# A macaron block of two mixtures of experts and a Mamba mixer: the odd pairs' sums are added to the even pairs' sums by an accumulating DMA, and the steps of the slots get a new order

## The chip, the cores and the metric

One core of one Trainium2 chip runs the whole program. The metric is the device time in microseconds; the median of the runs counts. The engines are TensorE (PE; its weight loads are PEld), VectorE (DVE), ScalarE (ACT), GpSimd (POOL) and SyncE (SP), which only issues transfers here.

## The reference

x is 16 sequences of 256 tokens of 128 values, all in fp32.

```python
x = x + 0.5 * ffn(layernorm(x))      # 8 experts 128 -> 512 -> 128, silu, top 2 of a softmax
x = x + attn(layernorm(x))
x = x + 0.5 * ffn(layernorm(x))      # the same weights

def attn(x):
    x1 = x + mamba(rmsnorm(x, norm1_w))
    out2 = memory_attend(mamba(rmsnorm(x1, norm2_w)))
    return x1 + out2

def mamba(x):                        # 256 channels, 16 states
    xm, res = split(x @ in_w.T + in_b)
    xm = silu(conv4(xm) + conv_b)
    delta = softplus(dt(xm)); Bm, Cm = parts(xm @ xp_w.T)
    h = h * exp(delta * A) + delta * xm * Bm     # a scan over 256 steps
    y = sum over the 16 states of h * Cm
    return ((y + xm * D_ssm) * silu(res)) @ out_w.T + out_b
```

What matters here is `y`: a sum over 16 states of products of 256 channels by 256 steps, plus `xm * D_ssm`.

## The kernel before

The 16 sequences go in 8 groups of two. Each sequence passes through Mamba twice, so a group has four scans. The time of one scan is a **slot**: 32 slots, q = 4g + i. Slots 0 and 1 of a group are the first pass of its two sequences, slots 2 and 3 the second. Beside the scan of its own sequence a slot does the end of the scan before it (its **tail**), the start of the next one (its **head**), and pieces of the experts' work for other groups: 35 pieces (transposing a chunk of sorted tokens T, first layer U, second layer D) are shared between slots 0 and 1 for one call of the experts, and between 2 and 3 for another. The first call and the last (`start`, `finish`) use every expert on every token instead.

In a slot the 16 states are taken as 8 pairs j of 128 x 1024 values (2 states x 2 halves of the channels x 256 steps). For a pair: ScalarE makes the decays (`d`, line 977; line 993 `e` scales the input of the odd pairs), TensorE spreads B and C over the partitions (`t`, `k`), VectorE forms the input of the even pairs (`b`, line 1332), scans (`s`, lines 1345 and 1351) and multiplies by C (`g`, line 1363). The products of pairs 0 and 1 are written to the tiles `acc[b]` and `odd[b]`, b = i % 2; those of pairs 2 to 7 go to three buffers G in turn. GpSimd adds each of these by an accumulating DMA of 512 KB: `a2`, `a4`, `a6` to `acc`, `a3`, `a5`, `a7` to `odd` (`pair_sum`, lines 1605 and 1608), each after the one before it on the same tile has landed. `skip` makes xm * D_ssm and adds it to `odd` too. The semaphores `q_even` and `q_odd` count the landings; `landed(q, j)` names the value for pair j.

In the next slot VectorE closes the tail with the step `gate` (`gate_y`, line 1366):

```python
dve.wait_ge(*landed(q, 6))
dve.wait_ge(*landed(q, 7))
V.tensor_tensor(acc[b], acc[b], odd[b], ALU.add)       # line 1370, 128x1024
V.tensor_tensor(yg, acc[b][:, 0], acc[b][:, 1], ALU.add)
V.tensor_tensor(yg, yg, sres[b], ALU.mult)
```

then TensorE projects `yg` (`out`, or `m1` to `m4` with the memory step), and VectorE adds the residual (`xsum` or `xb`). A product of pair j waits until its buffer G is free again, which is when the pair sum three before it has landed.

The routing of an experts' call stands in slots 1 and 3: `fstats` (VectorE), `froot` (GpSimd), `fnorm`, `fturn` (TensorE), `fxT` (ScalarE), `fgate` (TensorE), `flog ftop`, `fcount` (TensorE), `fplace`, which ends with the positions `posi` (line 1239). Then GpSimd scatters the tokens to DRAM in eight indirect DMAs (`sc0` to `sc7`, line 1560). In the same slots the call before comes to its end: ScalarE's last leaf F24 copies the last results to `ys` (line 898), SyncE stores them (line 407), GpSimd gathers them in eight indirect DMAs (`ga0` to `ga7`, line 1572, the first waits for all results), and VectorE adds the weighted sum `fsum` (line 1256) as the last step of the slot. `fkeep` is a copy of a tile on GpSimd (line 1553), `rms`, `lnx` and `rmsx` are small roots, `rs` a residual.

Every engine does its instructions in order. That order is written out by hand as the table `ORDER`: for each engine four strings, one for each slot of a group, of the names above (`p2`: two pieces; `F3`: leaf 3 of the experts' 25; `turned`, `r`, `xm`, `proj`, `sp`, `dx`: steps of the head; `oT`, `v`, `rT`: steps of the memory). ScalarE needs one table of functions for exp and ln and another for silu and tanh; wherever neighbours in the order differ, a table load (line 847) is issued.

## Time and profile before

| | us |
|---|---|
| median of 3 runs | 1679.26 (1675.97 to 1679.89) |
| the profiled execution's own time | 1679.97 |
| its span | 1678.1 |
| VectorE busy | 1391.7, 83% |
| TensorE busy | 1327.8, 79% |
| ScalarE busy | 1278.2, 76% |
| GpSimd busy | 650.4, 39% |
| granted TensorE clock, mean share | 0.904 |
| accumulating and indirect DMAs (queue 0) | 123.76 MB, 37.8% of 16 engines |

A share is the mean over 32 slots and the two ends; which engine ends a stretch must be read slot by slot. Slots follow each other at 41 to 55 us.

### The profile page before, as it was taken

What the parts mean: (1) busy time and instruction counts of PE and PEld (TensorE: products, weight loads), DVE (VectorE), ACT (ScalarE), POOL (GpSimd) and SP (SyncE); (2) the same over time, 40 slices, a digit from 0 to 9 for tenths busy, and PEclk for the clock granted to TensorE, in tenths of its full rate; (3) what the DMA queues carried; (4) which work ended last, traced back from release to release, by engine and by line L of the source; (5) the groups of instructions that cost most, each with busy time, mean ns of one, the idle gap of its engine ahead of it and who ended that gap; (6) DMA issues with size and microseconds to landing.
All of it is one profiled execution on the core that took longest, in us unless ns stands there. A gap on an engine that the chain in (4) does not pass through costs nothing. (4 is left out here: it accounts for less than half of the span.)

```text
span 1678.1 us, 29290 instructions
## 1 busy us (share of the span) xinstructions
PE 1327.8 (79%) x8754; PEld 1191.0 (71%) x8754; DVE 1391.7 (83%) x2149; ACT 1278.2 (76%) x2660; POOL 650.4 (39%) x681
## 2 busy tenths in 40 slices
PE   7978567878888787888878788877878787668778
PEld 6867456767777686777767687776867676457668
DVE  3367989989899888989889898989899888978742
ACT  3489658978788788979889797978889698548722
POOL 1212434263624536263523536263533534242220
PEclk9989769989989799988999899998999899768889
DMA  6336346676666667665666767665675765464631
GB/s 198 110 88 141 79 81 153 144 169 133 157 133 136 147 140 177 144 162 122 143 152 137 163 140 178 142 160 115 146 162 130 165 145 104 82 137 106 156 90 45
DMA packets 144231, 227.04 MB, mean 135 GB/s; under 512 B 13648, under 2 KB 79440, under 8 KB 143952
## 3 DMA queue, kind: packets, MB, share of 16 engines
q0 software_dynamic: 39424, 123.76, 37.8%
q1 hardware_dynamic: 104656, 101.41, 21.0%
q8 instruction: 77, 1.26, 0.3%
q14 instruction: 74, 0.61, 0.1%
HBM read 90.90 MB, written 25.17 MB: 69 GB/s over the span
## 5 line engine op out<-in xcount | busy, mean ns | idle before, releaser
L977 ACT ACTIVATE dA<-delta,A 128x255 f32<-128x255 f32 x1024 | 425.7, 495 | 5.3 <-DVE hs L1345 4.4
L1351 DVE TENSOR_TENSOR_SCAN hs<-dA,b_r 128x512 f32<-128x512 f32 x256 | 297.6, 1202 | 17.2 <-PE b_r L664 12.3
L1345 DVE TENSOR_TENSOR_SCAN hs<-dA,dbu 128x1024 f32<-128x1024 f32 x128 | 292.7, 2287 | 16.6 <-ACT dA L977 10.2
L539 PE MATMUL b_h<-xsT,wst 128*128 128x128 f32 x1680 | 253.7, 299 | 35.4 <-issue 28.6
L539 PEld LDWEIGHTS b_h<-xsT,wst 128*128 128x128 f32 x1680 | 227.2, 209 | 55.3 <-issue 53.4
L1363 DVE TENSOR_TENSOR G<-hs,b_r 128x1024 f32<-128x1024 f32 x192 | 233.3, 1215 | 33.1 <-PE b_r L675 27.6
L551 PE MATMUL b_out<-w2s,hT 128*128 x1680 | 234.8, 286 | 11.0 <-ACT ys L898 9.2
L847 ACT ACT_TABLE_LOAD x182 | 233.5, 1283 | 3.9 <-PEq L1751 0.7
L551 PEld LDWEIGHTS b_out<-w2s,hT 128*128 128x128 f32 x1680 | 215.8, 200 | 16.3 <-issue 14.8
L664 PE MATMUL b_r<-prm,scaled 128*128 128x128 f32 x1024 | 173.6, 300 | 57.0 <-ACT scaled L993 28.8
L993 ACT ACTIVATE scaled<-duT,dtT 128x256 f32<-128x256 f32 x512 | 217.0, 500 | 1.4 <-PE b_r L664 1.1
L664 PEld LDWEIGHTS b_r<-prm,scaled 128*128 128x128 f32 x1024 | 133.6, 156 | 73.1 <-DVE dbu L1332 30.3
L906 ACT ACTIVATE hT<-b_h 128x512 f32<-128x512 f32 x210 | 122.0, 595 | 70.8 <-PE b_h L539 69.6
L1608 POOL DMA_DIRECT2D odd<-G x96 | 90.2, 939 | 218.8 <-DVE G L1363 213.0
L675 PE MATMUL b_r<-bcr,selr 128*128 128x256 f32 x512 | 135.9, 349 | 48.0 <-DVE G L1363 26.3
L1560 POOL DMA_INDIRECT sorted<-xn,posi x112 | 146.3, 1306 | 62.3 <-DVE posi L1239 32.4
L1620 POOL DMA_DIRECT2D odd<-xd x32 | 29.0, 907 | 358.7 <-DVE odd L1363 308.1
L1332 DVE TENSOR_TENSOR dbu<-du,b_r 128x1024 f32<-128x1024 f32 x128 | 155.1, 1212 | 3.8 <-PE b_r L657 3.5
L1605 POOL DMA_DIRECT2D acc<-G x96 | 89.2, 930 | 171.1 <-DVE G L1363 153.8
L1572 POOL DMA_INDIRECT yk<-results,posi x112 | 128.1, 1144 | 36.3 <-issue 34.1
L604 PE MATMUL b_w<-uT,inx 128*128 128x256 f32 x512 | 139.2, 408 | 1.3 <-ACT uT L922 0.7
L675 PEld LDWEIGHTS b_r<-bcr,selr 128*128 128x128 f32 x512 | 87.7, 207 | 65.4 <-DVE G L1363 32.4
(179 smaller groups left out, 2256.1 us busy)
## 6 DMA issues: line engine op xcount, KB each, us to landing
wst<-w_dram SPq DMA_DIRECT2D x242, 256.0 KB
acc<-G POOLq DMA_DIRECT2D x96, 512.0 KB
odd<-G POOLq DMA_DIRECT2D x96, 512.0 KB
xsort<-sorted SPq DMA_DIRECT2D x70, 192.0 KB
results<-ys SPq DMA_DIRECT2D x70, 192.0 KB, 3.1
odd<-xd POOLq DMA_DIRECT2D x32, 256.0 KB
xin<-x_dram SPq DMA_DIRECT2D x8, 256.0 KB
sorted<-ys SPq DMA_DIRECT2D x2, 960.0 KB, 7.5
```

The lines of the kernel that those rows point to most:

```text
L539: last = mm(H[r % 2][:, w], wst[k % NW][:, w], xsT[i // CH % 2][:, t:t + P], start=True, stop=True)
L551: last = mm(Y[:, i % CH * D:(i % CH + 1) * D], hT[i % NH][:, c, :], w2s[:, e, c, :], start=c == 0, stop=c == HC - 1)
L664: last = nc.tensor.transpose(R[u % 2][:, h * T + t * P:h * T + (t + 1) * P], scaled[k % 2][:, d, t, h * P:(h + 1) * P], ident)
L675: last = mm(C[:, d * T:(d + 1) * T], selector(DS + DP * j + d), bcr[b][:, :], start=True, stop=True)
L847: nc.scalar.preload_act_table_set(name)
L977: last = do(dA[j % 4][:, d, k, 1:], delta[b][:, k, 1:], ACT.Exp, scale=A[:, k, s:s + 1])
L993: last = do(scaled[n % 2][:, d, t, :], duT[b][:, t, :], ACT.Identity, scale=dtT[b][:, s:s + 1])
L1332: V.tensor_tensor(dbu[n % 2][:, :, :, :], du[i % 2][:, :, :].unsqueeze(1).broadcast_to([P, DP, HALVES, T]), both(R[u % 2]).unsqueeze(2).br ...
L1345: V.tensor_tensor_scan(flat(hs[j % 2]), flat(dA[j % 4]), flat(dbu[n % 2]), 0.0, ALU.mult, ALU.add)\
L1351: V.tensor_tensor_scan(hs[j % 2][:, d, :, :].rearrange("p h t -> p (h t)"), dA[j % 4][:, d, :, :].rearrange("p h t -> p (h t)"), R[u % 2][ ...
L1363: V.tensor_tensor(to[:, :, :, :], hs[j % 2][:, :, :, :], both(C).unsqueeze(2).broadcast_to([P, DP, HALVES, T]), ALU.mult).then_inc(q_G, 1)
L1560: Q.indirect_dma_start(xs_d[m % 2], bass.IndirectOffsetOnAxis(ap=posi[m % 2][:, x:x + 1], axis=0), xn[:, j, :], None).then_inc(s_scat, 16)
```

## The change

`gate_y` no longer adds `odd` to `acc`. GpSimd does, with one more accumulating DMA, the step `w` (`merge`), for the tail's slot; VectorE waits for its landing. In the last group `merge` is called at the top of GpSimd's `finish`. All strings of `ORDER` are new; of the three longer tables the diff shows the fourth slot's strings.

```diff
@@ ORDER @@
 "tensor", slot 3
-t0 t1 p3 t2 k0 p2 t3 p2 fturn p2 fgate k1 p1 t4 fcount t5 p2 turng k2 p1 in k3 t6 p4 k4 t7 t8 xp dt k5 t9 t10 m1 t11 dx k6 m2 m3 k7 m4
+t0 p2 t1 t2 fturn k0 p3 fgate p2 k1 p1 t3 fcount p1 t4 k2 p1 turng p1 in t5 p1 k3 p2 t6 p1 k4 p1 t7 p1 xp t8 dt t9 k5 t10 m1 t11 dx k6 m2 m3 k7 m4
 "scalar", slot 3
-e1 F12 F13 d0 d1 F14 F15 e3 F16 F17 F18 fxT e5 F19 d2 d3 turned d4 F20 F21 ftanh F22 F23 r xm F24 d5 proj e7 sp d6 oT dx v d7 rT
+e1 F12 F13 d0 d1 F14 F15 fxT F16 F17 F18 e3 F19 d2 d3 turned F20 ftanh F21 d4 F22 e5 r F23 xm e7 F24 d5 proj sp d6 oT d7 dx v rT
 "vector", slots 0 to 3
-b0 s0 g0 s1 gate g1 b2 s2 g2 s3 low b4 g3 delta s4 g4 s5 b6 mask g5 s6 g6 s7 xb g7
-b0 fstats s0 s1 g0 fnorm b2 s2 flog ftop g1 fplace gate g2 s3 b4 xsum g3 un s4 g4 s5 g5 b6 fweights s6 g6 low s7 delta g7 fsum
-b0 s0 s1 g0 gate b2 g1 xsum s2 s3 un g2 b4 lx g3 s4 s5 g4 ln b6 low s6 g5 unx delta g6 s7 g7
-b0 fstats s0 s1 fnorm b2 g0 flog ftop g1 fplace s2 g2 s3 gate g3 b4 s4 fweights g4 s5 low g5 b6 delta s6 mask g6 s7 g7 xb fsum
+b0 s0 g0 s1 g1 gate b2 s2 g2 s3 b4 g3 low s4 delta s5 g4 mask b6 g5 s6 g6 s7 xb g7
+b0 fstats s0 s1 fnorm b2 g0 flog ftop g1 fplace gate s2 s3 xsum g2 b4 un g3 s4 s5 g4 b6 s6 fweights g5 g6 s7 low delta g7 fsum
+b0 s0 g0 s1 gate g1 b2 xsum s2 s3 un g2 b4 g3 lx s4 s5 ln g4 b6 low unx g5 s6 delta g6 s7 g7
+fstats b0 fnorm s0 s1 g0 flog ftop g1 b2 fplace s2 g2 gate s3 g3 b4 s4 g4 s5 g5 fweights low b6 delta s6 g6 mask s7 xb g7 fsum
 "gpsimd", slots 0 to 3
-skip a2 a3 a4 a5 a6 a7
-froot skip sc0 sc1 sc2 a2 sc3 sc4 fkeep rms a3 sc5 sc6 sc7 rs a4 ga0 ga1 ga2 ga3 a5 ga4 ga5 ga6 ga7 a6 a7
-skip rms rs a2 a3 lnx rmsx a4 a5 a6 a7
-froot skip sc0 sc1 sc2 a2 sc3 sc4 fkeep a3 sc5 sc6 sc7 a4 ga0 ga1 ga2 ga3 a5 ga4 ga5 ga6 ga7 a6 a7
+w0 a2 skip a3 a4 a5 a6 a7
+froot w0 skip sc0 sc1 sc2 sc3 sc4 rms sc5 a2 a3 sc6 ga0 sc7 a4 ga1 ga2 ga3 a5 ga4 ga5 ga6 rs ga7 a6 a7 fkeep
+w0 rms rs a2 skip lnx rmsx a3 a4 a5 a6 a7
+froot w0 skip sc0 sc1 sc2 sc3 sc4 sc5 a2 sc6 sc7 a3 a4 ga0 ga1 ga2 ga3 ga4 a5 ga5 ga6 ga7 a6 fkeep a7
@@ gate_y @@
                 q, b = 4 * g + i, i % 2
-                dve.wait_ge(*landed(q, 6))
-                dve.wait_ge(*landed(q, 7))
-                V.tensor_tensor(acc[b][:, :, :, :], acc[b][:, :, :, :], odd[b][:, :, :, :], ALU.add)
-                dve.drain()
+                dve.wait_ge(q_sum, (q + 1) * 16)
                 wait(dve, q_omm, q)
@@ gpsimd @@
+            def merge(g, i):
+
+                q, b = 4 * g + i, i % 2
+                pool.wait_ge(*landed(q, 6))
+                pool.wait_ge(*landed(q, 7))
+                Q.dma_start(flat(acc[b]), flat(odd[b]), accum_op=ALU.add).then_inc(q_sum, 16)
+
@@ slot of gpsimd @@
+                    elif name == "w":
+                        if tail:
+                            merge(*tail)
@@ finish of gpsimd @@
                 f = (LAST, xb, ob, GROUPS - 1, False)
+                merge(GROUPS - 1, 3)
                 ffn_root(LAST, one)
```

Line numbers of the new program are higher by 7 to 18 than those of the old one. The pieces are shared out anew: slots 0 and 1 had 16 and 19 of the 35, now 13 and 22; slots 2 and 3 had 18 and 17, now 19 and 16. The program has 182 table loads before and 214 after.

The gate on VectorE, at the change from slot 1 to slot 2 of group 4. Before:

```order
L1256 SCALAR_TENSOR_TENSOR xa<-yk,c,xa 128x128 x8
L1332 TENSOR_TENSOR dbu<-du,b_r 128x1024
L1345 SCALAR_TENSOR_TENSOR hs<-dA,dbu 128x1024
L1351 SCALAR_TENSOR_TENSOR hs<-dA,b_r 128x512 x2
L1363 TENSOR_TENSOR acc<-hs,b_r 128x1024
L1370 TENSOR_TENSOR acc<-acc,odd 128x1024
L1373 TENSOR_TENSOR yg<-acc 128x512
L1376 TENSOR_TENSOR yg<-yg,sres 128x512
L1332 TENSOR_TENSOR dbu<-du,b_r 128x1024
L1363 TENSOR_TENSOR odd<-hs,b_r 128x1024
```

Now:

```order
L1266 SCALAR_TENSOR_TENSOR xa<-yk,c,xa 128x128 x8
L1342 TENSOR_TENSOR dbu<-du,b_r 128x1024
L1355 SCALAR_TENSOR_TENSOR hs<-dA,dbu 128x1024
L1373 TENSOR_TENSOR acc<-hs,b_r 128x1024
L1361 SCALAR_TENSOR_TENSOR hs<-dA,b_r 128x512 x2
L1380 TENSOR_TENSOR yg<-acc 128x512
L1383 TENSOR_TENSOR yg<-yg,sres 128x512
L1373 TENSOR_TENSOR odd<-hs,b_r 128x1024
L1342 TENSOR_TENSOR dbu<-du,b_r 128x1024
```

The addition to `acc` is gone, the gate stands at the same place, and the second input (`dbu`) has moved behind the product to `odd`.

GpSimd in slot 3 of group 4, from the scatters to the end. Before:

```order
L1560 DMA sorted<-xn,posi 1920x128 x3
L1605 DMA acc<-G 128x1024
L1560 DMA sorted<-xn,posi 1920x128 x2
L1553 TENSOR_SCALAR xa<-xin 128x512
L1608 DMA odd<-G 128x1024
L1560 DMA sorted<-xn,posi 1920x128 x3
L1605 DMA acc<-G 128x1024
L1572 DMA yk<-results,posi 128x128 x4
L1608 DMA odd<-G 128x1024
L1572 DMA yk<-results,posi 128x128 x4
L1605 DMA acc<-G 128x1024
L1608 DMA odd<-G 128x1024
```

Now, with the merge that already belongs to the next slot as the last row:

```order
L1567 DMA sorted<-xn,posi 1920x128 x6
L1612 DMA acc<-G 128x1024
L1567 DMA sorted<-xn,posi 1920x128 x2
L1615 DMA odd<-G 128x1024
L1612 DMA acc<-G 128x1024
L1579 DMA yk<-results,posi 128x128 x5
L1615 DMA odd<-G 128x1024
L1579 DMA yk<-results,posi 128x128 x3
L1612 DMA acc<-G 128x1024
L1560 TENSOR_SCALAR xa<-xin 128x512
L1615 DMA odd<-G 128x1024
L1634 DMA acc<-odd 128x1024
```

The copy of `xin` has moved from among the scatters to between a6 and a7, and one more gather stands ahead of a5.

ScalarE in slot 3 of group 4, from the turned input (`uT`) to the last results (`ys`). Before:

```order
L922 ACTIVATE uT<-b_w 128x2x256
L977 ACTIVATE dA<-delta,A 128x255 x4
L847 ACT_TABLE_LOAD
L906 ACTIVATE hT<-b_h 128x512
L898 ACTIVATE ys<-b_out 128x384
L886 ACTIVATE th<-gap 128x4
L906 ACTIVATE hT<-b_h 128x512 x2
L934 ACTIVATE sres<-b_w,prm 128x256 x2
L943 ACTIVATE xm<-b_w,convb 128x256 x2
L898 ACTIVATE ys<-b_out 128x384
```

Now; the rows just ahead of these are as the first, third and fourth before (`uT`, a table load, one `hT`):

```order
L896 ACTIVATE th<-gap 128x4
L908 ACTIVATE ys<-b_out 128x384
L857 ACT_TABLE_LOAD
L987 ACTIVATE dA<-delta,A 128x255 x4
L857 ACT_TABLE_LOAD
L916 ACTIVATE hT<-b_h 128x512
L1003 ACTIVATE scaled<-duT,dtT 128x256 x4
L944 ACTIVATE sres<-b_w,prm 128x256 x2
L916 ACTIVATE hT<-b_h 128x512
L953 ACTIVATE xm<-b_w,convb 128x256 x2
L1003 ACTIVATE scaled<-duT,dtT 128x256 x4
L908 ACTIVATE ys<-b_out 128x384
```

The decays `dA` stand between two table loads of their own, and both scaling steps have come ahead of the last `ys`.

## Rows read from the trace of the kernel before

**Rows 1.** The page, part 1: busy us (share of the span) xinstructions, per engine.

```profile
PE 1327.8 (79%) x8754; PEld 1191.0 (71%) x8754; DVE 1391.7 (83%) x2149; ACT 1278.2 (76%) x2660; POOL 650.4 (39%) x681
```

**Rows 2.** Windows of group 4: length, busy us (xinstructions), granted clock, DMA share, GB/s.

```profile
851.40:893.90 42.50, 34.45 (x228) 30.20 (x228) 39.67 (x41) 36.23 (x75) 6.04 (x8) 0.92 0.61 134
893.90:913.10 19.20, 16.48 (x126) 15.02 (x125) 17.21 (x51) 17.98 (x32) 5.83 (x6) 0.95 0.50 121
913.10:945.60 32.50, 24.68 (x162) 21.91 (x160) 27.42 (x35) 22.35 (x48) 26.47 (x26) 0.92 0.74 175
945.60:990.40 44.80, 36.13 (x246) 33.76 (x247) 43.72 (x64) 39.61 (x83) 14.96 (x19) 0.89 0.60 128
990.40:1009.10 18.70, 15.96 (x125) 15.05 (x124) 14.93 (x48) 16.26 (x34) 5.84 (x6) 0.94 0.52 126
1009.10:1041.60 32.50, 27.01 (x182) 23.93 (x181) 28.41 (x28) 25.72 (x60) 26.00 (x24) 0.98 0.82 194
sum 190.20, PE 154.71 PEld 139.85 DVE 171.36 ACT 158.16 POOL 85.14; mean PE 25.79 PEld 23.31 DVE 28.56 ACT 26.36 POOL 14.19
```

**Rows 3.** Timeline of GpSimd, slot 3: start us, us, line, operation, out<-in, [idle before].

```profile
1009.50 2.86 POOL L1560 DMA_INDIRECT sorted<-xn,posi  x1 [1.75 <-DVE posi L1239]
...
1018.58 0.63 POOL L1553 TENSOR_SCALAR xa<-xin 128x512 f32<-128x512 f32 x1
...
1027.09 1.06 POOL L1572 DMA_INDIRECT yk<-results,posi  x1 [0.30 <-issue]
...
1037.25 0.95 POOL L1572 DMA_INDIRECT yk<-results,posi  x1 [0.30 <-issue]
...
1040.73 0.89 POOL L1608 DMA_DIRECT2D odd<-G  x1 [1.51 <-DMA odd<-G]
```

**Rows 4.** Lines, whole span: line, engine, operation, xcount | busy us, mean ns | idle before.

```profile
L847 ACT ACT_TABLE_LOAD x182 | 233.5, 1283 | 3.9 <-PEq L1751 0.7
...
L1370 DVE TENSOR_TENSOR acc<-acc,odd 128x1024 f32<-128x1024 f32 x32 | 38.8, 1212 | 0.1
```

**Rows 5.** Windows of 1 us round the pair sum issued at 968.36 (columns as rows 2).

```profile
968.00:969.00 1.00, 1.00 (x7) 1.00 (x6) 1.00 (x2) 0.75 (x3) 0.64 (x1) 0.50 0.00 0
969.00:970.00 1.00, 1.00 (x8) 0.94 (x7) 0.91 (x5) 1.00 (x4) 0.28 (x1) 0.90 0.33 66
...
972.00:973.00 1.00, 1.00 (x6) 0.87 (x6) 1.00 (x1) 1.00 (x1) 0.99 (x2) 1.00 0.38 70
```

**Rows 6.** Timeline of GpSimd: two odd pair sums, the second waits for the first's landing.

```profile
840.45 1.03 POOL L1608 DMA_DIRECT2D odd<-G  x1
...
850.29 0.89 POOL L1608 DMA_DIRECT2D odd<-G  x1 [2.65 <-DMA odd<-G]
```

**Rows 7.** Timeline round the change from slot 1 to 2: a7, weighted sum, gate.

```profile
945.33 0.89 POOL L1608 DMA_DIRECT2D odd<-G  x1 [0.44 <-issue]
...
945.60 3.12 DVE L1256 SCALAR_TENSOR_TENSOR xa<-yk,c,xa 128x128 f32<-128x128 f32 x8 [1.95 <-DMA yk<-results,posi]
...
955.52 1.22 DVE L1370 TENSOR_TENSOR acc<-acc,odd 128x1024 f32<-128x1024 f32 x1
```

**Rows 8.** Timeline of ScalarE, slot 3: the decays d4, a wait, F24 and a scaling step.

```profile
1011.54 1.69 ACT L977 ACTIVATE dA<-delta,A 128x255 f32<-128x255 f32 x4
...
1019.20 0.60 ACT L906 ACTIVATE hT<-b_h 128x512 f32<-128x512 f32 x1 [3.10 <-PE b_h L539]
...
1021.12 0.51 ACT L898 ACTIVATE ys<-b_out 128x384 f32<-128x384 f32 x1
...
1025.10 1.70 ACT L993 ACTIVATE scaled<-duT,dtT 128x256 f32<-128x256 f32 x4
```

**Rows 9.** Line 407, the results' transfer: min, median and max to landing.

```profile
DMA to landing us min/median/max: 2.1/3.1/7.2
```

**Rows 10.** Timeline of GpSimd at the end of the program.

```profile
1600.69 1.36 POOL L1608 DMA_DIRECT2D odd<-G  x1
1604.82 0.20 POOL L1536 TENSOR_TENSOR rstd<-mv,epst 128x2 f32<-128x2 f32 x1 [2.77 <-DVE mv L1095]
```

More of the change, by code:

```diff
@@ L111 @@
     "tensor": (
[4 rows of a table removed]
[8 rows of a table added]
     ),
     "scalar": (
[4 rows of a table removed]
[6 rows of a table added]
     ),
     "vector": (
[4 rows of a table removed]
[6 rows of a table added]
     ),
     "gpsimd": (
[4 rows of a table removed]
+        "w0 a2 skip a3 a4 a5 a6 a7",
+        "froot w0 skip sc0 sc1 sc2 sc3 sc4 rms sc5 a2 a3 sc6 ga0 sc7 a4 ga1 ga2 ga3 a5 ga4 ga5 ga6 rs ga7 a6 "
+        "a7 fkeep",
+        "w0 rms rs a2 skip lnx rmsx a3 a4 a5 a6 a7",
+        "froot w0 skip sc0 sc1 sc2 sc3 sc4 sc5 a2 sc6 sc7 a3 a4 ga0 ga1 ga2 ga3 ga4 a5 ga5 ga6 ga7 a6 fkeep "
+        "a7",
     ),
```

36 rows, old and new, of the table ORDER are left out of this document.

## Prediction, made before the changed kernel ran

> **What bounds the kernel now.** I read the page's busy line first: VectorE works 83% of the span, TensorE 79%, ScalarE 76%, GpSimd 39% [rows 1]. No engine is full on average, so I cut one round of four slots (group 4 of 8) at the two events that matter and took the windows [rows 2]. In them "g7" is a slot's last product, "positions" the end of the routing (`posi`), "weighted sum" the start of line 1256. The six stretches are one whole round, 190.20 us, and the reader should see three kinds:
>
> - weighted sum to the g7 of the next slot (42.50 and 44.80 us): VectorE busy 39.67 and 43.72. It is full, and 1 us taken from it is nearly 1 us.
> - g7 to positions (19.20 and 18.70 us): a chain of small steps through TensorE, ScalarE and VectorE, with VectorE idle 2.0 and 3.8 us.
> - positions to weighted sum (32.50 us twice): VectorE idles 5.1 and 4.1 us. Here GpSimd issues back to back: eight scatters, eight gathers, four pair sums. The gathers need the last results of the experts. The last gather starts at 1037.25, the weighted sum follows at 1041.6 [rows 3]. VectorE's surplus is worth nothing here.
>
> **What the change takes out.** 32 additions on line 1370 at 1.212 us: 38.8 us of VectorE [rows 4]. Each goes away in one slot's beginning. In slots 0 and 2 that lies in a stretch where VectorE is full. In slots 1 and 3 it lies behind the positions, in the GpSimd-bound stretch, and is worth 0 there; the cover is VectorE's idle 5.1 and 4.1 us, and without it 1.2 us more a slot would be gained. So at most 16 x 1.212 = 19.4 us of the 38.8 can show.
>
> **What it adds.** One accumulating DMA of 512 KB a slot. The trace has 192 of that size; GpSimd is held 0.9 us by one [rows 3], and none has its landing listed, so I bound it. Below: one alone, issued at 968.36 and its descriptors out at 969.3, moves bytes from 969 until within the slice 972 to 973, so about 4.1 us from the issue [rows 5]. Above: the one issued at 840.45 among gathers releases its successor at 850.29, 9.8 us [rows 6]. The new one runs in the quiet start of a slot and is nearest to the first, plus the tail until its semaphore is seen: I take 5. It starts only when the last odd pair sum has landed, and that one still runs beside gathers: 6 us, again nearer the low end.
>
> Slot 2: a7 of slot 1 starts at 945.33 and lands 6 on, the merge 5 on from there: 956.3. VectorE comes to the gate at 955.52 [rows 7]. So it waits 0.8 of the 1.2 it saved: -0.4 a slot. At the bounds (4.1 and 9.8 for either DMA) the wait is 0 or 9.4 us. Slot 0: the gate now stands behind one more product (1.2 us), and a7 starts at 1040.73, 0.9 before the weighted sum [rows 3]; the merge is in at 1040.73 + 11.1 = 1051.8, VectorE, as far from its weighted sum as in rows 7 (9.9) and one product more, at 1041.6 + 9.9 + 1.2 = 1052.7. No wait: -1.2. Slots 1 and 3 have the gate behind the routing, over 17 us after g7: no wait.
>
> In the queue of GpSimd the merge stands first (slots 0, 2) or after `froot` (1, 3) and holds what is behind it until a7 has landed: `rms`, `a2`, `skip`. Those wait for products that come later than that in slots 0, 1 and 3; in slot 2 `rms` is needed about 2 us after the gate and does not get late.
>
> **What the new order moves.** Three things touch a bound.
>
> (a) Slot 1, VectorE: scan s2 (2.3 us) moves from before the routing to behind the gate, so the positions come earlier by up to 2.3; the logits are then waited for, as in slot 3, whose stretch has 3.8 us of idle and not 2.0, and I keep half, -1.1. But a scatter, a4 and a residual move behind the first gather, by the like rows about 1.3 + 1.0 + 0.7 = 3.0 us of GpSimd [rows 3], against a first gather that can start about 2.2 earlier. Net +0.8 - 1.1 = -0.3; bounds -2.3 and +3.0.
>
> (b) Slot 3, ScalarE: before, the copy of the last results (F24) started 9.6 us after d4 did, 3 of them a wait for TensorE, which works on the projection there [rows 8]. Now three table loads (3.85, one of them as before [rows 4]), d4, e5 and e7 (1.7 each [rows 8]) and six short copies of about 0.6 stand between that point and F24: 3.85 + 5.1 + 3.6 = 12.5 us, with no time left to wait, so F24 is 2.9 later. Its transfer lands 3.1 us from issue in the median [rows 9]: before at 1021.1 + 0.5 + 0.5 + 3.1 = 1025.2, with the first gather at 1027.09 [rows 3] a slack of 1.9. So gathers, and the weighted sum, start 1.0 us later: +1.0. In the last two such slots no scatters stand ahead and the 2.9 counts in full. Bounds: -0.6 (only `fkeep`, 0.63 us [rows 3], leaves the way) and +2.9 everywhere.
>
> (c) The whole program has 214 table loads for 182: 32 x 1.283 = 41.1 us more ScalarE, as much as VectorE loses. In the fullest stretch, 44.80 us with ScalarE busy 39.61 [rows 2], slot 2's two more give 42.2, still below VectorE's 42.5. I take 0. ScalarE's idle time shows no drain at a switch: the row gives 3.9 us before 182 loads [rows 4]. The Trainium skill (ScalarE: Activation LUTs, What ACT_TABLE_LOAD costs) counts about 1.38 us of drain on top of 1.283. By that page 32 switches would be 85 us, slot 2's ScalarE 44.9, and its stretch would be about 2 us longer; the row speaks against it.
>
> **The end.** `finish` puts the merge ahead of the norm's root on GpSimd. Before, the root started at 1604.82, 4.1 us after a7 was issued [rows 10]. Now it waits for a7 to land (1600.69 + 6 to 6.8; I take the upper end, since a6 was issued 0.6 before it and both share the DMA engines) and for one issue (0.9): 1608.4, +3.6 us, and every step of the last experts hangs on it.
>
> **Sum.** Slot 0: 8 x -1.2 = -9.6. Slot 1: 6 x -0.3 = -1.8. Slot 2: 8 x -0.4 = -3.2. Slot 3: 5 x 1.0 + 2 x 2.9 = +10.8. End +3.6. Together -0.2 on the profiled execution's 1679.97 us; the median of the runs is 0.7 lower, 1679.3, so I say **1679**: no difference that a measurement can tell (0.3%, 5 us).
>
> **Rivals.**
>
> 1. *Faster*: the slack ahead of the first gather holds, and the positions come early. For it: F24's place depends on waits for TensorE that a new order may shorten, and in slot 1 it is now ahead of e7. Then slots 0 and 2 give 16 x -1.2, slot 1 7 x -1.1, the end +3.6: -23.3, 1656. Everything that line 1370 cost would be 1640.
> 2. *Slower, ScalarE becomes the engine that is waited for*: in slots 2 and 3 two more loads each, 2.6 us. It decides once ScalarE's own waits in slot 2 (5.2 us idle now [rows 2]) can't be closed up by more than half. Then scans wait for their decays: 14 such slots run experts: 14 x 2.6 = 36, less the 9.6 of slot 0, plus the end: +30, 1709. Against it: the idle time is there.
> 3. *Slower, the merge is late*: landing takes nearer 9.8 us than 5. The wait in slot 2 grows by 4.8 and one of 3.9 comes in slot 0: 8 x 8.7 = 70, 1751; with half the excess, 2.4 and 1.5 a slot, 1713. Against it: gathers are over when it runs.
> 4. *The DMA hides nothing because the addition was hidden anyway*: slots 0 and 2 turn out not to be full. Then only the end counts: 1683, within the forecast's range.
>
> **Chances.** Forecast (with rival 4), 1668 to 1691: 0.44, of which 0.10 is faster by over 5 us, 0.24 within, 0.10 slower. Rival 1: 0.29. Rival 2: 0.17. Rival 3: 0.10. So faster 0.39, same 0.24, slower 0.37. The range: 1650 leaves out the lower part of rival 1 (0.09), 1710 the upper ends of 2 and 3 (0.10). The forecast's own range is 1668 to 1691.
>
> **What would show it.** In the new profile: line 1370's row gone; VectorE's busy time down by 38.8 us; `yg` in slot 2 waiting 0.8 us for the DMA `acc<-odd`, in slot 0 not at all; 214 table loads; the stretch from positions to weighted sum in slot 3 33.5 us, not 32.5; the first stretch (weighted sum to g7, slot 0) 41.3, not 42.5; the root of the end 8 us after a7's issue. I am wrong if those stretches keep 32.5 while the gate doesn't wait (faster), or if scans wait for decays (`dA`) by more than a few us in total, or if the gate waits 3 us and more (slower).

## The result, and the profile after

| | before | after |
|---|---|---|
| median, us | 1677.7 (1675.97 to 1679.89, 4 runs) | **1708.57** (1706.67 to 1711.17, 4 runs) |
| ratio | | **1.0185**, 95% interval 1.0169 to 1.0201 |
| profiled execution, us | 1679.97 | 1709.48 |

The change makes the kernel 1.85% slower, 31 us. The forecast was no difference. (One of the ten executions of merge_only below, 1755.4 us at a granted clock of 0.72, is in its median but not in its ratio.) First the page's busy line, which answers to [rows 1], and its DMA part:

```profile
PE 1322.0 (77%) x8754; PEld 1185.0 (69%) x8754; DVE 1352.9 (79%) x2117; ACT 1324.8 (78%) x2692; POOL 675.2 (40%) x713
q0 software_dynamic: 44032, 140.54, 43.0%
acc<-odd POOLq DMA_DIRECT2D x32, 512.0 KB, 5.1
```

VectorE lost its 38.8 us, ScalarE has 46.6 us more, most of it table loads, and the new DMA lands 5.1 us after its issue in the median, as taken. None of this says where 31 us went. The windows of group 4, cut at the same events as [rows 2], do:

```profile
866.70:906.40 39.70, 32.27 (x229) 28.74 (x230) 38.17 (x39) 36.38 (x78) 6.98 (x9) 1.00 0.67 147
906.40:924.90 18.50, 16.55 (x129) 15.59 (x128) 15.09 (x49) 16.89 (x31) 6.78 (x7) 0.94 0.76 168
924.90:963.90 39.00, 29.69 (x185) 26.23 (x184) 27.83 (x35) 30.37 (x63) 27.28 (x25) 0.85 0.67 160
963.90:1008.50 44.60, 33.28 (x225) 30.55 (x226) 42.61 (x63) 36.62 (x72) 17.12 (x21) 0.89 0.63 137
1008.50:1024.90 16.40, 15.32 (x132) 14.67 (x131) 14.94 (x49) 14.46 (x29) 4.85 (x7) 1.00 0.82 185
1024.90:1059.00 34.10, 25.61 (x165) 22.22 (x164) 27.48 (x28) 29.00 (x64) 27.25 (x22) 0.95 0.74 174
```

Five of six stretches move by 0.2 to 2.8 us, mostly down. The third, slot 1 from the positions to the weighted sum, went from 32.50 to 39.00 us with VectorE as busy as before (27.42, 27.83): 6.5 us of new waiting. It is the same in all of groups 1 to 6 (39.0 to 39.4, before 32.3 to 33.1). VectorE waits for the gathered rows, 6.58 us where [rows 7] had 1.95:

```profile
963.87 3.05 DVE L1266 SCALAR_TENSOR_TENSOR xa<-yk,c,xa 128x128 f32<-128x128 f32 x8 [6.58 <-DMA yk<-results,posi]
```

Why they come late is in GpSimd's timeline of that stretch:

```profile
934.35 1.03 POOL L1567 DMA_INDIRECT sorted<-xn,posi  x1 [0.19 <-issue]
935.39 0.99 POOL L1612 DMA_DIRECT2D acc<-G  x1
936.44 0.88 POOL L1615 DMA_DIRECT2D odd<-G  x1
937.62 1.57 POOL L1567 DMA_INDIRECT sorted<-xn,posi  x1 [0.30 <-issue]
945.32 3.06 POOL L1579 DMA_INDIRECT yk<-results,posi  x1 [6.12 <-DMA results<-ys]
948.69 0.99 POOL L1567 DMA_INDIRECT sorted<-xn,posi  x1 [0.31 <-issue]
949.68 1.01 POOL L1612 DMA_DIRECT2D acc<-G  x1
...
960.41 0.96 POOL L1579 DMA_INDIRECT yk<-results,posi  x1 [0.16 <-issue]
```

The reader should see the 6.12 us ahead of the first gather, and that GpSimd waits there with a scatter and a4 still to be issued behind it. ScalarE had copied the last results at 937.48, so their transfer was issued at 938.0, 1.6 us after a3. It landed at 944.5, 6.5 us later; in groups 1 to 6 it took 6.7 us in the mean, before 3.8 (there the trace has only 3 to 5 of the 16 completions of each, so 3.8 is a lower bound). The DMA engines were full or nearly so all that while (0.87 to 1.14 in windows of 1 us; the DMA share stands before the last number):

```profile
937.00:938.00 1.00, 1.00 (x11) 1.00 (x11) 1.00 (x1) 0.49 (x1) 0.70 (x2) 1.00 1.05 205
...
941.00:942.00 1.00, 1.00 (x8) 0.89 (x7) 0.67 (x1) 0.98 (x3) 0.00 (x0) 1.00 1.14 220
...
944.00:945.00 1.00, 0.08 (x1) 0.00 (x0) 1.00 (x1) 1.00 (x4) 0.00 (x0) 1.00 1.06 407
```

Before, a2 and a3 were issued at 917.96 and 923.77 (4.8 and 10.7 us after the positions, now 10.5 and 11.5), so only one of them was near the transfer, 2.7 us ahead of it, and the first gather started with no wait. The share alone doesn't tell the two cases apart: it was 1.08, 0.95 and 0.94 from 926 to 929, too.

```profile
923.77 0.99 POOL L1608 DMA_DIRECT2D odd<-G  x1 [0.36 <-DVE G L1363]
...
930.27 1.00 POOL L1605 DMA_DIRECT2D acc<-G  x1
931.58 1.07 POOL L1572 DMA_INDIRECT yk<-results,posi  x1 [0.30 <-issue]
```

The lines of the whole span say the same: the wait of the gathers for the results rose from 1.9 to 47.6 us, and VectorE's for the gathered rows in `xa` (slot 1) from 14.5 to 45.4; in `ob` (slot 3) it fell from 15.7 to 5.4. The last row shows the gate's wait for the merge. Before:

```profile
L1572 POOL DMA_INDIRECT yk<-results,posi x112 | 128.1, 1144 | 36.3 <-issue 34.1 <-DMA results<-ys 1.9 <-DMA acc<-G 0.3
L1256 DVE SCALAR_TENSOR_TENSOR xa<-yk,c,xa 128x128 f32<-128x128 f32 x56 | 20.5, 427 | 15.0 <-DMA yk<-results,posi 14.5
L1256 DVE SCALAR_TENSOR_TENSOR ob<-yk,c,ob 128x128 f32<-128x128 f32 x56 | 18.6, 392 | 16.2 <-DMA yk<-results,posi 15.7
```

After:

```profile
L1579 POOL DMA_INDIRECT yk<-results,posi x112 | 133.7, 1194 | 78.2 <-DMA results<-ys 47.6 <-issue 30.3 <-DMA acc<-G 0.3
L1266 DVE SCALAR_TENSOR_TENSOR xa<-yk,c,xa 128x128 f32<-128x128 f32 x56 | 20.1, 420 | 45.9 <-DMA yk<-results,posi 45.4
L1266 DVE SCALAR_TENSOR_TENSOR ob<-yk,c,ob 128x128 f32<-128x128 f32 x56 | 15.9, 346 | 6.0 <-DMA yk<-results,posi 5.4
L1380 DVE TENSOR_TENSOR yg<-acc 128x512 f32<-128x512 f32 x32 | 22.2, 693 | 9.0 <-DMA acc<-odd 8.9
```

### The profile page after: what moved, and what is told of

It is laid out like the page before. It is cut to its first block and busy times, and to the rows that moved or that the text cites. A ratio compares the mean times of both kernels' runs of the same rounds, so it can differ in the third digit from the quotient of the medians.

```text
span 1707.7 us, 29321 instructions
## 1 busy us (share of the span) xinstructions
PE 1322.0 (77%) x8754; PEld 1185.0 (69%) x8754; DVE 1352.9 (79%) x2117; ACT 1324.8 (78%) x2692; POOL 675.2 (40%) x713
## 5 line engine op out<-in xcount | busy, mean ns | idle before, releaser
L1361 DVE TENSOR_TENSOR_SCAN hs<-dA,b_r 128x512 f32<-128x512 f32 x256 | 298.3, 1203 | 38.9 <-PE b_r L674 22.0
L1355 DVE TENSOR_TENSOR_SCAN hs<-dA,dbu 128x1024 f32<-128x1024 f32 x128 | 292.4, 2284 | 12.6 <-ACT dA L987 7.0
L549 PE MATMUL b_h<-xsT,wst 128*128 128x128 f32 x1680 | 245.8, 293 | 33.5 <-issue 18.8
L549 PEld LDWEIGHTS b_h<-xsT,wst 128*128 128x128 f32 x1680 | 219.8, 204 | 50.2 <-issue 48.4
L561 PE MATMUL b_out<-w2s,hT 128*128 x1680 | 233.7, 284 | 17.9 <-ACT hT L916 9.8
L674 PE MATMUL b_r<-prm,scaled 128*128 128x128 f32 x1024 | 170.5, 299 | 47.3 <-DVE dbu L1342 41.1
L1342 DVE TENSOR_TENSOR dbu<-du,b_r 128x1024 f32<-128x1024 f32 x128 | 155.2, 1213 | 35.2 <-PE b_r L667 33.0
L674 PEld LDWEIGHTS b_r<-prm,scaled 128*128 128x128 f32 x1024 | 135.5, 156 | 59.4 <-DVE dbu L1342 47.6
L1579 POOL DMA_INDIRECT yk<-results,posi x112 | 133.7, 1194 | 78.2 <-DMA results<-ys 47.6
L685 PEld LDWEIGHTS b_r<-bcr,selr 128*128 128x128 f32 x512 | 88.1, 211 | 75.0 <-DVE G L1373 37.4
L614 PEld LDWEIGHTS b_w<-uT,inx 128*128 128x128 f32 x512 | 96.1, 203 | 15.1 <-ACT uT L932 3.9
```

The lines of the kernel that those rows point to most:

```text
L549: last = mm(H[r % 2][:, w], wst[k % NW][:, w], xsT[i // CH % 2][:, t:t + P], start=True, stop=True)
L561: last = mm(Y[:, i % CH * D:(i % CH + 1) * D], hT[i % NH][:, c, :], w2s[:, e, c, :], start=c == 0, stop=c == HC - 1)
L614: last = mm(o, inx[:, m, r, ch], uT[:, b, PAD - r:PAD - r + T], start=r == 0, stop=r == PAD)
L674: last = nc.tensor.transpose(R[u % 2][:, h * T + t * P:h * T + (t + 1) * P], scaled[k % 2][:, d, t, h * P:(h + 1) * P], ident)
L685: last = mm(C[:, d * T:(d + 1) * T], selector(DS + DP * j + d), bcr[b][:, :], start=True, stop=True)
L1342: V.tensor_tensor(dbu[n % 2][:, :, :, :], du[i % 2][:, :, :].unsqueeze(1).broadcast_to([P, DP, HALVES, T]), both(R[u % 2]).unsqueeze(2).br ...
```

## The experiments

Theories: **A**, the new order of slot 1 costs it (two 512 KB pair sums right ahead of the results' transfer, more work behind the first gather); **B**, the merge DMA; **C**, the 32 more table loads. In the table, the slots are the times from one slot's last product to the next one's, means over groups 1 to 6; "slot 1b" is slot 1's stretch from the positions to the weighted sum, "gathers" the starts of the first and of the last gather after the positions. All from the timelines, in us. Each ratio is to the kernel before as timed beside that kernel (medians 1676.6 to 1679.0), so ratios compare better than medians.

| kernel | median | ratio (95%) | slots 0, 1, 2, 3 | 1b | gathers |
|---|---|---|---|---|---|
| before | | 1 | 44.2, 49.6, 47.6, 47.9 | 32.8 | 18.5, 30.1 |
| after | 1708.6 | 1.0185 | 40.5, 50.7, 52.1, 49.7 | 39.1 | 20.7, 35.5 |
| merge_only | 1679.6 | 1.0016 (0.9997–1.0035) | 43.4, 49.8, 47.1, 49.0 | 32.3 | 17.8, 28.9 |
| order_only | 1718.5 | 1.0239 (1.0215–1.0263) | 41.5, 51.8, 50.9, 50.4 | 39.0 | 21.2, 35.6 |
| old_01 | 1684.7 | 1.0044 (1.0023–1.0065) | 42.1, 49.5, 47.0, 49.9 | 32.0 | 17.7, 28.8 |
| old_23 | 1709.4 | 1.0190 (1.0167–1.0214) | 42.0, 50.8, 52.2, 48.0 | 38.4 | 20.8, 35.2 |
| pairs_behind_gather | 1715.6 | 1.0218 (1.0179–1.0258) | 41.2, 52.1, 51.3, 51.0 | 37.8 | 16.1, 34.7 |
| slot1_pool_old | 1718.6 | 1.0245 (1.0209–1.0281) | 41.1, 53.5, 49.2, 50.3 | 37.7 | 23.3, 35.1 |
| slot1_dve_old | 1716.7 | 1.0229 (1.0193–1.0265) | 40.9, 52.7, 50.5, 50.9 | 37.4 | 20.0, 34.5 |
| slots01_pe_act_old | 1785.0 | 1.0634 (1.0597–1.0672) | 44.5, 61.2, 46.8, 51.0 | 41.4 | 20.6, 35.5 |
| slot1_spread | 1700.3 | 1.0154 (1.0119–1.0190) | 40.9, 52.7, 47.5, 50.7 | 35.8 | 17.4, 33.0 |
| spread_f24 | 1704.5 | 1.0180 (1.0145–1.0216) | 40.5, 52.9, 47.3, 51.6 | 36.2 | 17.4, 33.3 |
| spread_f24_end | 1702.2 | 1.0157 (1.0130–1.0184) | 40.4, 52.8, 47.5, 52.1 | 36.0 | 17.4, 33.2 |
| slot1_both_old | 1705.0 | 1.0171 (1.0143–1.0199) | 40.8, 52.5, 47.0, 50.8 | 33.0 | 19.0, 30.1 |
| slot1_g2_early | 1692.4 | 1.0078 (1.0051–1.0105) | 40.5, 52.2, 47.1, 50.7 | 34.5 | 19.5, 31.1 |
| merge_old_end | 1674.9 | 0.9977 (0.9961–0.9993) | 44.6, 49.5, 47.1, 48.1 | 32.2 | 17.7, 28.9 |
| merge_half | 1681.1 | 1.0011 (0.9995–1.0027) | 43.7, 49.3, 47.9, 48.0 | 33.0 | 18.6, 30.4 |

The last gather says more than the first: where it starts at 29 to 31, the stretch takes 32 to 34.5 us, where it starts at 33 and later, 35.8 us and more, and the first can be the earliest of all (16.1) in a slow kernel.

One string in the diff ahead of the prediction is not that of the changed kernel: TensorE's new slot 3 has `k4 t7 p1 xp`, 16 pieces, and not `k4 p1 t7 p1 xp`.

### Splitting the change: DMA or order, and which slots

**merge_only**: the changed kernel with the old table, and `w0` put in.

```diff
-    (all new strings)
+    (all old strings, but on GpSimd:)
+        "w0 skip a2 a3 ...",  "froot w0 skip sc0 ...",  "w0 skip rms rs a2 ...",  "froot w0 skip sc0 ..."
```

> The merge by DMA, with the old order of steps. Theory A (the new order of slot 1 puts two pair sums directly ahead of the results' transfer and three more operations behind the first gather; the merge itself costs nothing): slots 0 and 2 gain up to 1.2 us each, the end loses 1 to 4, so 1660 to 1677 us, against 1677.7 before. Theory B (the merge costs: its 512 KB a slot slow the other accumulating and indirect DMAs, or hold GpSimd's queue): most of the change's +31 us is here, 1695 to 1710, and the stretch from the positions to the weighted sum of slot 1 is 36 us and more. Theory C (32 more table loads on ScalarE): here there are 182 again, so also 1660 to 1677.

1679.6 us, no difference that can be told. The 32 more DMAs cost nothing that shows (B is out) but gain nothing either, so Theory A's and C's time (1660 to 1677) was missed too; below comes why.

**order_only**: the kernel before with the new table, without `w0`.

```diff
-    (all old strings)
+    (all new strings, "w0" left out)
```

> The new order of steps with the addition kept on VectorE, without the merge. Theory A: the whole loss of the change and the additions that the merge would have saved in slots 0 and 2 on top (1.2 us x 16 at most): 1708 to 1728 us; slot 1's stretch from the positions to the weighted sum stays at 39 us. Theory B: the loss goes away, 1672 to 1690. Theory C: as A in total (1708 to 1728), but the lost time lies in stretches where scans wait for decays, and slot 1's stretch falls with nothing.

1718.5: the order costs 40 us, of which the merge gives 10 back (1.2 us in slot 0, 0.3 in slot 2, by the stretches' means). Slot 1's stretch is 39.0 us without any merge DMA.

**old_01** and **old_23**: the changed kernel with the old strings, `w0` put in, of slots 0 and 1, or of 2 and 3, on all four engines.

```diff
-    (new strings of slots 0 and 1)      # old_23: of slots 2 and 3
+    (old strings of slots 0 and 1, with w0)
```

> The changed kernel with the old order in slots 0 and 1. Theory A: slot 1's stretch behind the positions goes back from 39.1 us to about 33, slot 0 loses some of its gain (2.9 us to about 1.2): 1708.6 - 6 x 6 + 8 x 1.7 + 6 x 0.7, about 1690 us (1683 to 1697). Theory B: no change, 1703 to 1713. Theory C (slots 0 and 1 carry no more table loads of the 32 than slots 2 and 3): a third to half of the loss back, 1693 to 1700, and slot 1's stretch stays above 36.

> The changed kernel with the old order in slots 2 and 3. Theory A: the three stretches of slots 2 and 3 are -0.5, -2.3 and +1.7 us against before, so undoing them changes little: 1703 to 1716 us. Theory B: no change, 1703 to 1713. Theory C: both additional loads of slots 2 and 3 are gone, 1685 to 1700.

1684.7 and 1709.4: of the 31 us, 24 come back with slots 0 and 1, none with 2 and 3, and slot 1's stretch goes to 32.0. C is out by the lines of the table loads, first of old_01, then of old_23:

```profile
L847 ACT ACT_TABLE_LOAD x212 | 272.0, 1283 | 4.5 <-PEq L1759 0.7
```

```profile
L847 ACT ACT_TABLE_LOAD x184 | 236.1, 1283 | 4.0 <-PEq L1759 0.7
```

The first has 30 of the 32 additional loads and not the time, the second has the time and 2 of the loads.

### What in slot 1

**pairs_behind_gather**:

```diff
-froot w0 skip sc0 sc1 sc2 sc3 sc4 rms sc5 a2 a3 sc6 ga0 sc7 a4 ga1 ...
+froot w0 skip sc0 sc1 sc2 sc3 sc4 rms sc5 sc6 ga0 a2 a3 sc7 a4 ga1 ...
```

> The changed kernel, but in slot 1 GpSimd issues a2 and a3 behind the first gather and not right ahead of the results' transfer. Theory A (those two fill the DMA engines, so that the results land 7 us after issue and not 3, and the first gather waits 6 us): the results land about 3 us after issue, the first gather starts 3 to 4 us earlier (17 instead of 21 us after the positions), slot 1's stretch falls from 39.1 to 35 or 36, and the run takes 1684 to 1694 us. Theory D (the last results are late for another reason, so the place of a2 and a3 means nothing): 1703 to 1713. Theory E (a2 and a3 later keep the three buffers full, and the products g5 and g6 wait): the gather comes earlier, but the gain is lost, 1700 to 1715.

The transfer's part came out as Theory A says: issued at the same place (13.2 us after the positions), it landed 2.1 us later in the mean of six groups and not 6.7, and the first gather started at 16.1 instead of 20.7. But the stretch is 37.8 and the run not faster at all (1715.6, 0.6 above Theory E's range). GpSimd's timeline of group 4:

```profile
950.73 0.99 POOL L1569 DMA_INDIRECT yk<-results,posi  x1 [4.44 <-DMA results<-ys]
951.72 1.02 POOL L1602 DMA_DIRECT2D acc<-G  x1
952.36 1.32 POOL L1605 DMA_DIRECT2D odd<-G  x1
953.98 1.06 POOL L1557 DMA_INDIRECT sorted<-xn,posi  x1 [0.30 <-issue]
958.50 0.89 POOL L1602 DMA_DIRECT2D acc<-G  x1 [3.46 <-DMA acc<-G]
959.70 1.04 POOL L1569 DMA_INDIRECT yk<-results,posi  x1 [0.30 <-issue]
```

a4 now waits for a2's landing at the head of the queue, and seven gathers wait behind it. None of the three theories had this wait. Theory E's wait is there too: VectorE's products wait 13.0 us in all for landed pair sums, and the gate waits 20.0 us for the merge (8.9 in the changed kernel).

**slot1_pool_old**, **slot1_dve_old** and **slot1_both_old**: the changed kernel with the old string of GpSimd, of VectorE, or of both, in slot 1 alone.

```diff
# vector, slot 1 (dve_old, both_old)
-b0 fstats s0 s1 fnorm b2 g0 flog ftop g1 fplace gate s2 s3 xsum g2 b4 un g3 ...
+b0 fstats s0 s1 g0 fnorm b2 s2 flog ftop g1 fplace gate g2 s3 b4 xsum g3 un ...
# gpsimd, slot 1 (pool_old, both_old)
-froot w0 skip sc0 sc1 sc2 sc3 sc4 rms sc5 a2 a3 sc6 ga0 sc7 a4 ...
+froot w0 skip sc0 sc1 sc2 a2 sc3 sc4 fkeep rms a3 sc5 sc6 sc7 rs a4 ga0 ...
```

> The changed kernel with GpSimd's old string in slot 1 alone. Theory A: VectorE's new string makes the product g2 only about 8 us after the positions, so a2, third behind the scatters there, holds five scatters and the first gather: that one stays at 20 to 22 us after the positions, but nothing but gathers follows it, so the stretch falls only from 39.1 to 36 to 38 and the run takes 1695 to 1706. Theory F (GpSimd's string alone is at fault): 33 us and 1672 to 1688.

> The changed kernel with VectorE's old string in slot 1 alone. Theory A: a2 and a3 stay where GpSimd's string has them, right ahead of the results' transfer, so the stretch stays at 38 to 39.5 us, and the one before it loses 0.5 to 0.7: 1706 to 1716. Theory G (VectorE's string, which brings g2 and g3 late, is at fault by itself): 1672 to 1690.

> The changed kernel with the old strings of both VectorE and GpSimd in slot 1. Each alone left the stretch at 37.4 to 37.7 us. Theory A (the two belong together: g2 early on VectorE lets a2 go early on GpSimd): a2 at 4 to 5 us after the positions, the first gather at 18, the stretch 33 to 35 us, 1685 to 1702. Rival (TensorE's and ScalarE's new strings in slots 0 and 1 carry the loss): 37 and more, 1706 to 1720.

Alone, neither helps: the stretch stays at 37.7 and 37.4 us. With GpSimd's old string a2 waits until 8.8 us after the positions, because VectorE's new string makes g2 late, and the first gather starts at 23.3. For GpSimd's string the stretch was foreseen, the first gather (20 to 22) and the run (13 us over the range) were not. With VectorE's string the stretch is 0.6 us under what was expected, and the one before it grew to 20.3 us where it should have shrunk; the run is 1 us over its range. Both together bring it to 33.0, with a2 at 4.2 us, so the two strings belong together. But the run takes 1705, 3 us over the range, and its ratio, 1.0171, can't be told from the change's 1.0185. The stretch comes back and the time doesn't: the stretch before it takes 20.4 us (18.8 in the changed kernel, 19.2 in old_01, which has TensorE's and ScalarE's old strings too), the gate waits 16.1 us for the merge and not 8.9, and the scans 26.6 us for TensorE and not 22.0. That TensorE's order, written for the new VectorE order, is the reason was not tried by itself.

**slots01_pe_act_old**: TensorE's and ScalarE's old strings in slots 0 and 1.

```diff
-(new strings of tensor and scalar, slots 0 and 1)
+(old strings of tensor and scalar, slots 0 and 1)
```

> The changed kernel with the old strings of TensorE and ScalarE in slots 0 and 1. Theory A: the last leaf may come 1 to 2 us earlier, but its transfer is issued beside a2 and a3 all the same: stretch 37 to 39 us, 1698 to 1712. Rival (the pieces and leaves of the new strings come late): stretch 33 to 35, 1675 to 1692.

Both missed: 1785. F24 came 4.5 us later (17.1 after the positions), not earlier, and scans waited 78.7 us for TensorE's spread input (38.9 in all for that line in the changed kernel, 22.0 of it for TensorE):

```profile
L1351 DVE TENSOR_TENSOR_SCAN hs<-dA,b_r 128x512 f32<-128x512 f32 x256 | 300.5, 1205 | 94.2 <-PE b_r L664 78.7 <-ACT dA L977 11.3 <-issue 3.8
```

It says that strings of different tables do not fit, and nothing on which table is better.

**slot1_spread**:

```diff
-froot w0 skip sc0 sc1 sc2 sc3 sc4 rms sc5 a2 a3 sc6 ga0 sc7 a4 ga1 ga2 ga3 a5 ga4 ga5 ga6 rs ga7 a6 a7 fkeep
+froot w0 skip sc0 sc1 sc2 sc3 sc4 rms sc5 a2 sc6 sc7 ga0 ga1 a3 ga2 a4 ga3 ga4 a5 ga5 ga6 ga7 rs a6 a7 fkeep
```

> The changed kernel; in slot 1 GpSimd issues a2 early, both last scatters, then the first two gathers, then a3, and a4 and a5 spread among the gathers, so that nothing large is issued just ahead of the results' transfer and no pair sum waits at the queue's head for the one before. Theory A: results land 2 to 3 us after issue, the first gather starts 16 us after the positions and the last before 29; then VectorE's last product (32 us after the positions in the changed kernel) is what the weighted sum waits for: 33 to 34 us for the stretch instead of 39.1, and 1668 to 1684 us. Rival (slot 1's new order loses the time by VectorE's and TensorE's own waits): 37 and more, 1695 to 1710.

1700.3, a ratio of 1.0154: 5 us better than the change, with intervals that overlap. It lies in the rival's range, and the stretch, 35.8 (3.3 of the 6.3 us back), between the two. The results landed 3.4 us after issue, with one pair sum ahead of them; the first gather came at 17.4. Group 4:

```profile
935.74 1.00 POOL L1569 DMA_INDIRECT yk<-results,posi  x1 [1.18 <-DMA results<-ys]
...
947.41 0.99 POOL L1605 DMA_DIRECT2D odd<-G  x1 [3.40 <-DVE G L1363]
...
951.34 1.03 POOL L1569 DMA_INDIRECT yk<-results,posi  x1 [0.31 <-issue]
```

Now a5 (the second row) holds three gathers, and the last gather starts at 33, not before 29 as expected. The profile puts a5's wait down to a product, but its own, g5, had been done since 942.9; what was still out was a3's landing, for which VectorE's g6 waited too:

```profile
941.72 1.21 DVE L1363 TENSOR_TENSOR G<-hs,b_r 128x1024 f32<-128x1024 f32 x1
946.18 1.22 DVE L1363 TENSOR_TENSOR G<-hs,b_r 128x1024 f32<-128x1024 f32 x1 [3.25 <-DMA odd<-G]
```

Such waits of products for a landing are 21.4 us in all (none in the changed kernel). The gathered rows in `xa` are waited for 10.0 us only, less than before the change (14.5), and the last product is done 34.1 us after the positions (31.9 in the changed kernel, 30.4 before).

**slot1_g2_early**: slot1_spread with two more moves, one in VectorE's string and one in GpSimd's (the diff is against slot1_spread).

```diff
-gate s2 s3 xsum g2 b4 un g3                                  # vector, slot 1
+gate s2 g2 s3 xsum b4 un g3
-... sc3 sc4 rms sc5 a2 sc6 sc7 ga0 ga1 a3 ga2 a4 ga3 ...     # gpsimd, slot 1
+... sc3 a2 sc4 rms sc5 a3 sc6 sc7 ga0 ga1 a4 ga2 ga3 ...
```

> As slot1_spread, but in slot 1 VectorE makes the product g2 directly behind scan s2 (and not behind s3 and the residual), and GpSimd issues a2 among the scatters, a3 before the last two, a4 behind the second gather. Theory A (what is left of slot 1's loss, 35.8 us against 32.8, is that a2 and so the whole chain of pair sums starts 5 us late, which makes the last gathers wait for a3's landing): the stretch falls to 32.5 to 34 us and the run takes 1676 to 1688, against 1700 for slot1_spread. Rival (what is left is VectorE's work moved behind the positions and its waits for TensorE): the last product stays 32 us and more after the positions, the stretch 34.5 to 36, 1692 to 1702.

1692.4 and 34.5 us, at the lower edge of the rival's ranges. The interval lies below slot1_spread's, so the late chain of pair sums did cost something: 1.3 us of the stretch, and no product waits for a landing any more. In the last 1.7 us, VectorE's last product is done 33.7 us after the positions (mean; 30.4 before), so there its own work behind the positions and its waits decide, as the rival has it. The first gather started 2.1 us later than in slot1_spread, with a3 right ahead of the results' transfer, which landed 4.4 us after its issue, and the kernel was faster all the same.

### Slot 3, the end, and why the merge gains so little

**spread_f24** and **spread_f24_end**:

```diff
-... r F23 xm e7 F24 d5 ...        # scalar, slot 3, on slot1_spread
+... r F23 xm F24 e7 d5 ...
# spread_f24_end: for the last slot VectorE adds acc and odd, and in finish
-                merge(GROUPS - 1, 3)
```

> As slot1_spread, and in slot 3 ScalarE copies the last results (F24) 1.7 us earlier, ahead of the scaling step e7. Theory P (slot 3's gathers set the weighted sum, as the prediction had it): slot 3's stretch shortens by 1 to 1.7 us, 5 to 10 us in all, against slot1_spread. Theory V (in slot 3 VectorE's last product is the last to come, 33.2 us after the positions, while the last gather is issued at 28.7): no change, within 3 us of slot1_spread.

> As spread_f24, and the last slot's tail alone is done the old way: VectorE adds the two tiles and GpSimd's finish has no merge. The time from the last product to the end was 78.5 us before and 79.9 to 81.0 with the merge: 1.3 to 2.5 us less than spread_f24, and the best of all kernels here if Theory A holds, 1664 to 1682. Rival: the end doesn't hang on it, 0.

The swap brings nothing (1704.5 and 1700.3, ratios 1.0180 and 1.0154 with overlapping intervals), but it hardly tests Theory P: F24 moved from 14.2 to 13.9 us after the positions in the mean and not by 1.7, and the first gather of slot 3 not at all (19.2 and 19.7). Theory V rests on the traces. In the changed kernel's slot 3 the first gather is even a little earlier than before (17.4 us after the positions for 17.9), though F24 is 1.7 us later in group 4: `fkeep` (0.6 us) has left the way, and the results' transfer, now with no pair sum in the 4 us ahead of it, lands in 2.3 us. The last gather starts at 28.9 us in both. What ends slot 3 is VectorE's last product at 33.0 to 33.9 us (before 29.0 to 30.1). The end's merge costs 2 us: from the last product to the end of the span 76.1 us without it, 78.2 with it. That spread_f24_end would be the fastest of all rested on Theory A's number for slot1_spread, and fell with it.

**merge_old_end** and **merge_half**: merge_only with the last slot's tail on VectorE; and the same with the DMA only for the tails that slots 0 and 2 close.

```diff
+                if q == 4 * GROUPS - 1:      # merge_half: if q % 2 == 0 or q == 4 * GROUPS - 1
+                    V.tensor_tensor(acc[b], acc[b], odd[b], ALU.add)
...
-                merge(GROUPS - 1, 3)
```

> merge_only (the merge by DMA with the old order) with the last slot's tail done the old way, so without the merge in GpSimd's finish. From the last product to the end merge_only's profile shows 81.0 us and before's 78.6; 2 us of it go: about 1675 to 1678 us. Theory S (of the 38.8 us of additions only those in the full stretches count): round by round as merge_only, which gained 0.7 us a slot 0 and gave as much back in slot 3. Rival: the end is not the place where merge_only lost its gain: 1679 to 1681.

> As merge_old_end, but only the tails closed in slots 0 and 2 use the DMA; in slots 1 and 3 VectorE adds as before. Theory S (an addition in slots 1 and 3 is hidden, as the prediction had it, and a merge there holds GpSimd's queue ahead of skip): equal to merge_old_end or up to 5 us better, 1669 to 1677. Theory T (without the addition in slot 1 the product g2 is 1.3 us earlier, a2 with it and the scatters behind it 0.9 us earlier, so an addition there is worth 0.5 to 0.9 us a slot): 3 to 7 us slower than merge_old_end, 1678 to 1684.

merge_old_end, 1674.9 us, beats both kernels: 0.9977 (0.9961 to 0.9993), 4 us under before. merge_half, at 1.0011, is some 6 us (0.0034) slower, in Theory T's range. Without the addition the slot 1 product g2 ends 2.5 us after the positions, not 3.8, a2 is issued at 4.2 for 4.8, the first gather starts at 17.7 for 18.6, and the stretch is 32.2 for 33.0. The intervals do not overlap, if only by 0.0002. The two profiled executions don't show the 6 us: the one of merge_old_end took 1678.9 us and that of merge_half 1674.3, and there 0.8 us of slot 3's stretch to the positions goes the other way. So the 0.8 us in slot 1 is seen, and that it makes the whole difference is not.

## Why the prediction was wrong, step by step

- **The removed additions**: right in VectorE's busy time, wrong in their worth. "Worth 0" in slots 1 and 3 fails in slot 1: the gate stands ahead of g2, g2 releases a2, and a2 stands ahead of scatters in GpSimd's queue; with the old order 0.8 us of 1.2 came through (merge_old_end beside merge_half).
- **Slots 0 and 2**: the landing of the merge (5.1 for 5), that of a7 (at most 6.8 for 6 in group 4) and the gate's wait (1.0 for 0.8) were right; [rows 7] answer to this:

```profile
975.06 0.69 DVE L1380 TENSOR_TENSOR yg<-acc 128x512 f32<-128x512 f32 x1 [1.03 <-DMA acc<-odd]
```

 Slot 2's stretch lost 0.2 us in group 4 (predicted 0.4). Slot 0's was 2.8 us shorter instead of 1.2: 1.2 is the merge, as order_only shows, the rest the new order, where VectorE idles 1.5 us and not 2.8.
- **The step that failed: (a), slot 1.** The first half held in its direction: g7 to positions went from 19.3 to 18.8 us in the mean of groups 1 to 6, -0.5 for -1.1. The second, +0.8 with 3.0 as the upper bound, measured +6.3. Of its terms, what moves behind the first gather was sized right: from the first to the last gather it is 3.2 us more, for 3.0. The other, a first gather 2.2 us earlier, was wrong: it starts 2.2 us later (20.7 for 18.5). No row stands beside that 2.2. With a quiet transfer it holds, since pairs_behind_gather has the first gather 2.4 us earlier; but the prediction never followed the last results' transfer, which that gather waits for. F24 did not get earlier (12.6 us after the positions, before 12.5), and the transfer was priced at its median where it was priced at all; [rows 9] had 7.2 as its maximum, and the order's list showed a2 and a3 moving next to it. The last 0.9 us, from the last gather to the weighted sum, had no term. So +6.3 less 0.5 in six slots, 35 us, stands where -1.8 stood. That alone is more than the miss of 30. (The profiled span grew by 29.6 us: groups 1 to 6 by 21.9, in which the other stretches save 13 of these 35, group 0 by 7.8, the end by 1.3, and group 7 is 1.4 shorter.) old_01 returned 24 us, since it gives up part of slot 0's gain too. Behind the gathers stands a second loss that they hide in the changed kernel: VectorE's last product is 1.6 us later. So undoing the transfer's delay alone gave no time back (pairs_behind_gather, where a4's wait took its place), and how the 35 us divide between the two pair sums ahead of the transfer and the rest of slot 1's order stays open.
- **(b), slot 3**: +1.0 per slot was measured as +1.7 in this stretch, but for another reason, and with -2.3 in the one before. F24's chain was costed about right (12.3 us for 12.5 in group 4; it began 1.0 us sooner after the positions, so F24 is later by 1.7 and not 2.9), yet it did not reach the gathers. VectorE's own work had moved behind the positions. Slot 3's two stretches together, in group 4: 50.5 us, before 51.2.
- **(c), ScalarE**: right in its worth, 0, though not in its size: in slot 2's long stretch ScalarE is busy 36.62 us, less than before, and not 42.2. 214 loads, 4.5 us of idle time ahead of them all (before 3.9 for 182), and old_01 has 30 of them without the loss. The Trainium skill (ScalarE: Activation LUTs, What ACT_TABLE_LOAD costs) adds a drain of about 1.38 us to each switch; no row here shows one:

```profile
L857 ACT ACT_TABLE_LOAD x214 | 274.6, 1283 | 4.5 <-PEq L1769 0.7
```

- **The end**: +3.6 foreseen; from the last product to the end it is +1.3 in the changed kernel, +2.4 in merge_only, 2 in the pair spread_f24. The mechanism is right, and the root came 7.1 us after a7's issue for 7.7 by the prediction's terms, but not all of that reached the end: the merge, and with it the root, waits for a7 ([rows 10] answer to these).

```profile
1628.11 0.90 POOL L1615 DMA_DIRECT2D odd<-G  x1 [0.56 <-DVE G L1373]
1634.60 0.85 POOL L1634 DMA_DIRECT2D acc<-odd  x1 [5.59 <-DMA odd<-G]
1635.16 0.52 POOL L1543 TENSOR_TENSOR rstd<-mv,epst 128x2 f32<-128x2 f32 x1
```

- **Rivals**: rival 2 gave 1709 and the run took 1708.6, but by coincidence; its waits (scans for decays) are 19.8 us in all after, 11.9 before, so 8 us and not 36, though that is more than the "few us" that the prediction named as its sign. Rival 3 did not happen: the gate waits 8.9 us in all. (Its own terms give 1749 and 1710 and not 1751 and 1713; nothing hangs on that.) None of the four had a transfer that becomes slow because of what is issued ahead of it. The range reaches to 1710 for the sake of rivals 2 and 3, so that it holds the measured time is luck.
- **Still open**: group 0 ends 7.8 us later than before, 2 of them in its first slot. With the old strings in slots 0 and 1 it is 2.5, so most goes with those strings (one wait of 6.8 us for the results stands in it). The rest was not followed up, nor was group 6, where slot 2 takes 53.7 us (51.2 to 52.4 in groups 1 to 5) and slot 3 doesn't shorten as it did before (49.4 us, before 44.3).
